# Four moves in the schedule of a fused recurrent block: outer products in two buffers, earlier projections and norm, a later feed forward, all keys normed on VectorE

## What is computed

```
xn = layernorm(x)
s = attention(xn)         # 16 heads of 64, causal softmax over 256 tokens, times Wo
g = silu(moe(xn))         # 8 experts, top 1, and a shared feed forward of 352
x = x + s * g
xn = layernorm(x)
s = linear_attention(xn)  # 16 heads of 8: q . cumsum(k (x) v) / (q . cumsum(k)), phi = elu + 1
g = silu(local(xn))       # 2 layers: token shift, qkv, l2 norm of q and k, rotary, window 64,
x = x + s * g             #           then norm, gated feed forward of 341
```

## Time and profile before

| | us |
|---|---|
| median of 3 runs | 2106.64 (2105.45 to 2107.70) |
| profiled execution | 2113.86, of which the trace's span is 2112.1 |
| rounds of 36 ticks at 584.2, 820.3, 1054.5, 1291.2 | 236.1, 234.2, 236.7, 234.3 |
| ticks before the first round (to 359.2); first round (359.2 to 584.2) | 359.2; 225.0 |
| last round (1525.5 to 1771.7); two last blocks (1771.7 to 2112.1) | 246.2; 340.4 |

### The profile page before, as it was taken

The page is one execution under the profiler, slowest core; times in us unless marked ns, Lnnn a source line. Parts: engine busy times, 40 slices in busy tenths (PEclk is TensorE's granted clock), DMA queues, the critical chain, the costliest instruction groups (busy, mean ns, idle before and its releaser), DMA issues.

```text
span 2112.1 us, 38035 instructions
## 1 busy us (share of the span) xinstructions
PE 1783.7 (84%) x12532; PEld 1147.1 (54%) x12532; DVE 1255.7 (59%) x4179; ACT 1187.6 (56%) x3527; POOL 895.2 (42%) x1025
## 2 busy tenths in 40 slices
PE   6679989997989889987989889987989798685876
PEld 4358754663565456654465456554565455363554
DVE  4434447556666556656766556656766656867653
ACT  2444547655656665666666565566566565553643
POOL 2633216523643245423553255414653255647510
PEclk9889999999999989999999999999999997787978
DMA  8146500000000000000000000000000000000000
GB/s 234 45 157 208 189 16 5 8 1 1 6 2 16 1 1 6 17 1 1 6 1 16 1 1 7 16 1 1 6 2 11 1 6 1 1 6 0 1 1 11
DMA packets 49725, 53.49 MB, mean 25 GB/s; under 512 B 6386, under 2 KB 42236, under 8 KB 49532
## 3 DMA queue, kind: packets, MB, share of 16 engines
q0 software_dynamic: 7808, 27.79, 4.0%
q1 hardware_dynamic: 41724, 23.26, 3.9%
HBM read 41.60 MB, written 9.44 MB: 24 GB/s over the span
## 4 chain that ended last, share of the span: by engine, by line
PE 46%; DVE 12%; issue 10%; ACT 7%; POOL 7%; DVEq 0%; ACTq 0%; POOLq 0%
PE ps L650 5%; PE ps L608 4%; PE ps L588 4%; PE ps L547 4%; PE ps L725 3%; PE ps L567 3%; PE ps L632 3%; PE ps L767 2%; PE ps L776 2%; PE ps L769 2%; PE ps L622 2%; POOL xn L308 2%; POOL big L1447 2%; DVE p L1033 2%; POOL big L1446 1%
## 5 line engine op out<-in xcount | busy, mean ns | idle before, releaser
L1333 POOL COPY rdx<-rden 128x256 f32<-128x256 f32 x256 | 99.5, 418 | 599.9 <-DVE rden L1050 574.9
L1033 DVE CUSTOM_DVE_ANT_0 p<-ps,mask 128x128 f32<-128x128 f32 (+1 forms) x512 | 152.2, 353 | 249.8 <-PE ps L580 215.3
L1033 DVE CUSTOM_DVE_ANT_0 p<-ps,mask,nrq 128x128 f32<-128x128 f32 x512 | 149.0, 347 | 204.1 <-PE ps L576 203.4
L588 PE MATMUL ps<-ident,p 128*128 128x128 f32 x1280 | 221.4, 297 | 26.8 <-ACT p L865 23.9
L865 ACT ACTIVATE p<-p,nmax 128x128 f32<-128x128 f32 (+1 forms) x512 | 226.4, 442 | 0.0
L725 PE MATMUL ps<-wqkv,hT 128*128 128x512 f32 x384 | 197.4, 623 | 27.9 <-ACT big L944 27.7
L864 ACT ACTIVATE p<-p,nmax 128x128 f32<-128x128 f32 x512 | 200.3, 391 | 34.5 <-DVE nmax L1033 34.0
L879 ACT ACTIVATE pt<-ps 128x384 f32<-128x384 f32 (+1 forms) x256 | 111.7, 436 | 185.2 <-PE ps L588 184.6
L588 PEld LDWEIGHTS ps<-ident,p 128*128 128x128 f32 x1280 | 143.8, 147 | 107.0 <-issue 89.2
L1446 POOL TENSOR_TENSOR big<-big,rots 128x512 f32<-128x512 f32 x64 | 99.6, 1556 | 206.0 <-ACT big L944 206.0
L557 PE MATMUL ps<-ident,big 128*128 128x128 f32 x512 | 90.9, 317 | 93.3 <-DVE big L1228 47.6
(11 more groups left out here) (251 smaller groups left out, 4207.7 us busy)
## 6 DMA issues: line engine op xcount, KB each, us to landing
slots_in<-xn SPq DMA_DIRECT2D x1, 2560.0 KB, 14.0
v<-slots_in SPq DMA_DIRECT2D x20, 128.0 KB, 4.6
slots_out<-v SPq DMA_DIRECT2D x20, 128.0 KB, 1.9
big<-in_x SPq DMA_DIRECT2D x4, 512.0 KB, 6.1
x<-in_x SPq DMA_DIRECT2D x8, 256.0 KB, 3.0
out_x<-x SPq DMA_DIRECT2D x8, 256.0 KB, 2.3
wqkv<-in_wqkv SPq DMA_DIRECT2D x2, 768.0 KB
xn<-in_x SPq DMA_DIRECT2D x6, 256.0 KB, 3.2
```

What stands on the lines that cost most here:

```text
L588: last = nc.tensor.transpose(bank[:, j * P:(j + 1) * P], c.p[:, u % 4, j * P:(j + 1) * P], c.ident[:, :])
L1033: last = V.tensor_tensor_reduce(out=c.p[:, u % 4, a:b], in0=bank[:, a:b], in1=mask, scale=scale, scalar=3e38, op0=ALU.add, op1=ALU.min, ac ...
```

## The change

Seven edits, of which the first four are in `Plan`:

- `kv` and `cum`: tiles 2 and 3 of `kv`, at ticks +6 and +7 after the local attention's first, go to +5; the first sequence's last two `cum` go from +3, +4 to +5, +6, their sums one tick later each.
- `xload`, `xn` and `xnT` of blocks 3 to 7: 14, 14 and 12 ticks earlier. `v` is split by tile: half 0 from one tick two before its first use to two ticks 11 and 10 before it; half 1 from a tick shortly before use to two tiles one tick before the block's first step, two 7 after it.
- `ffn` of blocks 3 to 6: from the three ticks ahead of `down0` to ticks 8, 7 and 6 before `comb`; `wo` of half 1 three ticks later; `down0` one tick earlier, `comb` stays. Block 2's `ffn`, `down0` and `comb` all go five ticks earlier.
- `ln1` and `ln1n` of blocks 1 to 6: 8 ticks earlier.
- The second sequence's outer products get a home of their own: the half of `big` that holds `c.qkr` (for the two last blocks the weights of the first attention, now one tensor `w0`). Tile 2 waits for the last turned keys in place of `cum`.
- `kn` is all on DVE; POOL's `kn` is gone.
- `v`'s ring names get the tile.

```
-            self.put(a, "ln1", b)
-            self.put(a + 1, "ln1n", b)
+            self.put(a - (8 if 0 < b < LAST else 0), "ln1", b)
+            self.put(a - (7 if 0 < b < LAST else -1), "ln1n", b)
...
-            for t, at in enumerate((-1, 0, 6, 7)):
-                self.put(l0 + at, "kv", b, t)
-            for n in range(2 * LPARTS):
-                at = l0 + 1 + n + 4 * (n >= LPARTS)
-                self.put(at, "cum", b, n // LPARTS, n % LPARTS)
-                self.put(at + 1, "sum", b, n // LPARTS, n % LPARTS)
+            for t in range(2):
+                self.put(l0 - 1 + t, "kv", b, t)
+            for n, at in enumerate((1, 2, 5, 6, 9, 10, 11, 12)):
+                self.put(l0 + at, "cum", b, n // LPARTS, n % LPARTS)
+                self.put(l0 + at + 1, "sum", b, n // LPARTS, n % LPARTS)
+                if n == 2:
+                    for t in range(2, TILES):
+                        self.put(l0 + at, "kv", b, t)
...
+            held.append((f0 - 5, f0 - 3) if b < XRING else (f0 - 19, f0 - 15))
...
-            if b:
-                self.put(f0 - 2, "v", b, 0)
-            self.put(f1 - 3, "v", b, 1)
+            for t in range(TILES):
+                if b:
+                    self.put(f0 - (2 if b < XRING else 11 - t // 2), "v", b, 0, t)
+                self.put(f1 - 3 if b < XRING else f0 - 1 if t < 2 else f0 + 7, "v", b, 1, t)
+            late = 4 if XRING <= b < LAST else 0
             for half in range(2):
-                self.put(self.end[(0, b, half, PAIRS - 1)] + 4, "wo", 0, b, half)
-            c = max(self.end[(0, b, 1, PAIRS - 1)] + 4, e_end + 3)
+                self.put(self.end[(0, b, half, PAIRS - 1)] + 4 + (late - 1 if late and half else 0), "wo", 0, b, half)
+            c = max(self.end[(0, b, 1, PAIRS - 1)] + 4, e_end + 3) + late
...
-                self.put(c - 3 + ch, "ffn", b, ch)
+                self.put(c - 3 - late + ch, "ffn", b, ch)
...
             self.put(c, "down0", b)
-            self.put(c, "comb", b)
+            self.put(c + (late > 0), "comb", b)
...
-    c.kv = [a[:, 0:2 * LH * LD * LE].rearrange("p (t n) -> p t n", t=2) for a in homes]
+    seconds = [big[:, 4096:8192]] * (LAST - 1) + [w0] * 2
+    c.kv = [[a[:, 0:2 * LH * LD * LE].rearrange("p (t n) -> p t n", t=2) for a in ab] for ab in zip(homes, seconds)]
...
-        for t in range(KN_VECTOR):
+        for t in range(TILES):
             k_over_norm(V, c, t).then_inc(c.kn_ready, 1)
...
+        elif t == 2 and b < LAST - 1:
+            pool.wait_ge(c.mm_full, last_keys(plan, mm, plan.turn[(b, 0)]))
         elif t == 2:
-            pool.wait_ge(c.mm_full, mm.full("cum", b, 0, LPARTS - 1, 0))
-            pool.wait_ge(c.prod_ready, 4 * LPARTS * b + 2 * LPARTS)
+            pool.wait_ge(c.mm_full, mm.full("k", last_pair(plan, 0, LAST, 1)))
...
-        for t in range(KN_VECTOR, TILES):
-            k_over_norm(G, c, t).then_inc(c.kn_ready, 1)
```

More of the change, by code:

```diff
@@ L44 @@
 RSQRT_MAGIC = 1597463007.0
-KN_VECTOR = 2
 class Common:
@@ L981, in scalar @@
         evacuate(c.xnT[:, i, :] if i < 2 else c.xrT[i % 2], "rT", i)
-    values_of_tokens(0, 0)
+    for t in range(TILES):
+        values_of_tokens(0, 0, t)
     produce(0, plan.step(0))
```

64 lines of the change are left out of this document (31 added, 33 removed), and 2 rows, old and new, of the table USES.

## The result

| | before | changed |
|---|---|---|
| median of the runs, us | 2107.17 (2105.45 to 2109.18) | 2093.42 (2090.82 to 2096.84) |
| ratio, 95% interval | | 0.9935 (0.9918 to 0.9953) |
| the same pair on another chip (below) | 2116.72 | 2097.13, ratio 0.9903 (0.9884 to 0.9922) |
| span of the profiled execution | 2112.1 | 2095.0 |

The change makes the kernel faster by 14 to 20 us. The forecast was 30.5. It named the direction, but the time, 2093, is that of its rival "the clock takes it back", and the traces show that it came about mostly in another way.

What follows compares the result with a forecast made beforehand. PE was taken to set the pace, with 30 us idle per round. At −5.7 us a round, −23 for four rounds, +1, −6, +0.5 and −3 elsewhere gave −30.5, so 2076 us; range 2048 to 2098.

Steps and rivals of the forecast that it cites:

- the clock takes it back: Moved work behind PE's remaining waits runs at half clock: round −1.5, total −13.5 us, time 2093; chance 0.20.
- second norm, two of `v`, both `cum`: Around 859: `ln2n` 1.9 us faster without `cum`, two value matmuls add 2.3; +1.0 there, +0.3 for the other `cum`.
- `v` behind `wo` of half 0: Four value matmuls leave the place behind `wo`, where nothing waits: −3.6 us a round.
- turns, `kn`, first `v`: At 974 to 983, value matmuls fill two waits and four `kn` on DVE finish before POOL did: −2.3 us.
- `ln1n`, `ffn`: At 991 to 1008: the 1.59 us wait for POOL's whitening goes (−1.6), six feed-forward matmuls come in (+5.2).
- two `rot` ticks and the roots: Before `rr`, chunk 0 and `xnT` leave (−3.2 on PE), but DVE is nearly the bound: −2.6 us.
- Around `rr`: At the reciprocal roots: tick stays 11.1 us, idle becomes about 4; behind it `down0` costs 0, half clock +0.5.
- DVE takes the place of PE: From 991 to 1046, ticks without `wo` and chunk 0 don't shorten: total +10 us, time 2117; chance 0.08.
- The first round: Block 2's feed forward and `down0` in new ticks, without the `v` gain or a crowded `ln2n`: +1 us.
- The stretch up to the first round: Before the first round, four `kn` instead of two delay one mask: +0.5 us.
- The last round and the last two blocks: Last round −6 us (`v`, `cum`, `kn`, `ln1`, delayed last norm); last two blocks −3 (`cum` moved, four `kn` on DVE).
- Its signs: Expected: `ln2n` 2.3 to 2.7 us, rounds 226 to 231; wrong if `kn` exceeds 3 us or clock falls below 0.94.

Runs made afterwards that it cites:

- `comb_late`: The changed kernel with the residual update `comb` of blocks 3 to 6 one tick later; ratio to the kernel before 0.9827.
- `wo_150`: The changed kernel with `wo` of half 1 one tick earlier, ahead of the last `rot`; ratio to the kernel before 0.9970.
- `late_undone`: The changed kernel with `ffn`, `wo` of half 1 and `down0` of blocks 3 to 6 back at their old places; ratio to the kernel before 0.9896.
- `kn_split`: The changed kernel with `kn` of tiles 2 and 3 back on POOL; ratio to the kernel before 0.9912.
- `three`: The changed kernel with `comb` a tick later, two value matmuls a tick earlier, block 0's outer products (tiles 2, 3) at +6, +7; ratio to before 0.9775.
- `cum_alone`: The changed kernel with the first sequence's last two `cum` at +3, +4 and tiles 2 and 3's outer products at +6, +7; ratio to before 0.9898.
- `five_124`: `three` with the value matmuls of tiles 2 and 3 ahead of the second norm's turn, not behind it; ratio to the kernel before 0.9675.

## Why the prediction was wrong

Point by point, in the round from 820.3 us (measured from the starts of the masks; in us):

| place | forecast | measured |
|---|---|---|
| second norm, two of `v`, both `cum` | +1.3 | +0.8 |
| `v` behind `wo` of half 0 | −3.6 | −3.5 |
| turn at 919 | 0 | +2.2 |
| `xnT` | +0.8 | +0.5 |
| turns, `kn`, first `v` | −2.3 | −2.5 |
| `ln1n`, `ffn` | +3.6 | +2.4 |
| `wo` of half 1 out of its tick | −3.4 | −3.9 |
| two `rot` ticks and the roots | −2.6 | −1.1 |
| behind the roots, to the next outer products | +0.5 | +2.9 |
| sum | −5.7 | −2.2 |

- **The failing step is "Around `rr`", +0.5 where +2.9 was measured.** "`down0` moves forward by a tick (0)" followed only PE: `comb` on DVE, in the same tick as before, no longer had to wait for `down0` and so came forward onto POOL's outer product. The rule was at hand, it had priced `ln2n`, but I asked it only of the instructions that the diff takes away, not of those that move. By `comb_late` it is 3.3 us a round, so without the collision the step would have come out at −0.4, the edge of its bounds. The half clock behind the wait, priced within 0.5, costs 1.3 us on `down0` alone (4.20 against 2.94), but it is not what made the step fail.
- **"Two `rot` ticks" −2.6 was too much**: from there DVE's chain sets the pace, as `wo_150` and `late_undone` show, and PE's freed time became wait (1.1 us won of 2.6). The prediction's own rival "DVE takes the place of PE" was true there, in part.
- **The turn at 919** was not in the sum. I took one round for all, 820.3, and it was one of the two that kept their clock at this place. The mean of the four, 235.3, was in the table. Against that mean the four rounds gained 3.9 us each.
- **`kn`, the right amount for the wrong reason.** `kn` on DVE brings 0.9 us of the 2.5 (`kn_split`), the rest goes by the trace to the value matmuls.
- **The first round**, +4.1 and not +1: I counted the moved work there but not that POOL's queue had 7 us in one piece ahead of a spreading, in short ticks. `three` and `cum_alone` give it back. Block 2's `down0`, now in this round, is covered: with it `three` takes 224.2 us, less than the 225.0 before.
- **The stretch up to the first round**, +3.0, isn't the change's doing: kernels that are the same there took 359.4 (`comb_late`) to 362.2 us (changed). 1.4 us of this lie behind a wait of 7.6 us, where the clock is 0.61 from 310.5 to 318.0 in the changed kernel and 0.80 in the same stretch of `comb_late`, and 1.6 us at 343.5, where it is 0.66 for 5 us in the changed kernel and 1.00 in `comb_late`. Of the 17.1 us between the two profiled executions this hides about 3.
- **The last round and the last two blocks** came out as forecast (−6.2, −2.5), in part by luck. The last round has a `comb` collision that the forecast didn't count, and has lost a `down0` to the round ahead of it, which it didn't count either. The last two blocks hold 4.8 us of loss that `cum_alone` gives back.
- **The rival at 2093** gave the time, by a sum of half clock at 859 (+1.1), behind the roots (+1.5) and at the keys (1.6). At 859 PE did run at half clock (3.24 us for the two value matmuls, 1.88 at full clock in `five_124`), but the place as a whole came out below the forecast (+0.8 for +1.3), and so did the keys; about 1.3 are measured behind the roots, and 2.2 at a place that it did not name, in two rounds of four. The collision of DVE and POOL at `comb` costs 13 us in its four places, as much as the whole forecast missed; better figures elsewhere (`ffn`, `wo`) made up for the rest. The Trainium skill ("TensorE: Matmul & The Clock Gate", HAM oscillation), on which it leaned, describes a wait in each turn of a loop with the lower clock behind it. The trace agrees at 1041.77 (0.60 behind 3.73 us) and at 918 (0.54 behind 2.8 us); in the kernel before the same wait of 2.8 us was followed by full clock in one round and 0.60 in the next.
- **Its signs.** The steps of `ln2n`, the waits, `kn`'s four (2.84 us) and the last 340 us came as it said. Three of the four rounds are longer than the 231 us it allowed, and one sign of being wrong came: in the round from 1052.9 the clock's share is 0.93, which the kernel before has in one round too.

## What to carry to other kernels

When work is moved, follow every operation that moves with it on each engine, and look what the other engine of a shared port has running at the new time: the DVE operation waits for what is left of the POOL instruction, whatever its own size, and the next one for the next POOL instruction. A gate on POOL handed that price here to the next DVE piece, twice. A wait that another engine's chain makes went away here neither by reordering the chain's last link nor by taking work out ahead of it; put independent matmuls into it, ahead of the waiting instruction. Take the base of a sum from several turns of a loop, since one turn can be the lucky one, and read a gain at the place that was edited: the mean round also moves with the clock at places that no edit touched.
